# Queries and values of an edge-attention layer made by one 256-column product in three rotating PSUM banks

## What is computed

```python
Xq = (H @ W_lin.T).reshape(bt, n, h, dh)
Xv = (H @ W_val.T).reshape(bt, n, h, dh)
e = jnp.einsum('behd,hd->beh', jax.nn.leaky_relu(Xq[:, src] + Xq[:, dst], 0.2), a)
e = e + jnp.log(A0[src, dst] + EPS)[None, :, None]
# softmax of e over the edges of each source node gives attn
Vt = Xv[:, dst].transpose(1, 0, 2, 3)
Y = jax.ops.segment_sum(attn[..., None] * Vt, src, num_segments=n)
return Y.transpose(1, 0, 2, 3).reshape(bt, n, d) @ W_out.T
```

## Time and profile before

| | us |
|---|---|
| median of 3 runs | 1201.16 |
| lowest to highest | 1200.19 to 1201.65 |
| the profiled execution | 1202.18 |
| its span, first to last instruction | 1200.4 |
| TensorE busy in the span | 1161.4 |
| VectorE busy | 991.0 |
| ScalarE busy | 817.9 |
| mean granted TensorE clock | 0.994 |

### The profile page before, as it was taken

One profiled execution on the slowest core, in us unless ns is written; L12 is line 12 of the kernel. 1 busy time (PEld: TensorE's weight loads), 2 busy tenths in 40 slices (PEclk: granted clock), 3 DMA queues, 4 the chain that ended last, 5 costly groups with the idle time before them and its releaser, 6 DMA issues. The chain is left out here.

```text
span 1200.4 us, 23784 instructions
## 1 busy us (share of the span) xinstructions
PE 1161.4 (97%) x7820; PEld 1021.9 (85%) x7820; DVE 991.0 (83%) x2791; ACT 817.9 (68%) x1826; POOL 387.9 (32%) x717
## 2 busy tenths in 40 slices
PE   5999999999999999999998999989999999999998
PEld 4798898998988989889897898877777798889997
DVE  5888988888889888898886899988877689976665
ACT  4685886868868768588685777757777777753332
POOL 4211100100001001010011677756666487742332
PEclk9999999999999999999998999999999999999999
DMA  9400000000000000000000000000000000002222
GB/s 261 121 1 1 1 2 0 0 0 0 0 0 0 0 0 0 0 0 0 1 1 1 2 2 2 2 1 1 2 1 1 1 2 1 2 3 69 71 69 73
DMA packets 26306, 20.85 MB, mean 17 GB/s; under 512 B 1776, under 2 KB 22256, under 8 KB 26224
## 3 DMA queue, kind: packets, MB, share of 16 engines
q1 hardware_dynamic: 25648, 19.68, 5.8%
q10 hardware_dynamic: 576, 0.13, 0.1%
HBM read 11.42 MB, written 8.39 MB: 17 GB/s over the span
## 5 line engine op out<-in xcount | busy, mean ns | idle before, releaser
L554 ACT ACTIVATE gate<-ps,b_lstm 128x256 f32<-128x256 f32 (+2 forms) x624 | 309.5, 564 | 94.4 <-PE ps L581 92.9
L579 PE MATMUL ps<-H_hi,w_hi 128*128 128x256 f32 (+2 forms) x624 | 210.3, 338 | 1.9 <-DVE H_lo L470 1.2
L580 PE MATMUL ps<-H_hi,w_lo 128*128 128x256 f32 (+2 forms) x624 | 205.1, 330 | 0.0
L581 PE MATMUL ps<-H_lo,w_hi 128*128 128x256 f32 (+2 forms) x624 | 193.2, 330 | 0.0
L131 POOL TENSOR_SCALAR rstd<-mv 128x8 f32<-128x8 f32 x16 | 5.0, 311 | 500.3 <-DVE mv L111 500.1
L579 PEld LDWEIGHTS ps<-H_hi,w_hi 128*128 128x128 f32 x624 | 117.7, 189 | 15.8 <-DVE H_lo L470 3.2
L580 PEld LDWEIGHTS ps<-H_hi,w_lo 128*128 128x128 f32 x624 | 117.9, 189 | 8.1
L581 PEld LDWEIGHTS ps<-H_lo,w_hi 128*128 128x128 f32 x624 | 115.4, 189 | 10.1 <-DVE H_lo L508 1.5
L579 PE MATMUL ps<-hid_hi,w_hi 128*128 128x256 f32 (+2 forms) x384 | 120.5, 320 | 0.3
L580 PE MATMUL ps<-hid_hi,w_lo 128*128 128x256 f32 (+2 forms) x384 | 116.8, 311 | 0.0
L561 ACT ACTIVATE tanh_c<-cell 128x512 f32<-128x512 f32 (+2 forms) x176 | 90.9, 516 | 24.5 <-DVE cell L498 17.4
(11 more groups left out here) (205 smaller groups left out, 3095.6 us busy)
## 6 DMA issues: line engine op xcount, KB each, us to landing
out<-x SPq DMA_DIRECT2D x32, 256.0 KB, 2.3
x<-in_WihT SPq DMA_DIRECT2D x1, 768.0 KB, 11.3
x<-in_WhhT SPq DMA_DIRECT2D x1, 768.0 KB, 6.0
x<-in_x_in SPq DMA_DIRECT2D x2, 256.0 KB, 3.6
x<-in_x_in SPq DMA_DIRECT2D x1, 512.0 KB, 7.9
x<-in_WihT SPq DMA_DIRECT2D x1, 256.0 KB, 8.2
tanh_c<-in_WqkvT SPq DMA_DIRECT2D x1, 192.0 KB, 5.0
w_sb<-in_W SPq DMA_DIRECT2D x1, 192.0 KB, 4.2
```

The source lines that it names most:

```text
L554: nc.scalar.activation(gate[:, g, z, 0:w * GB], gate_bank(g, k, m)[:, 0:w * GB], ACT.Tanh if z == G else ACT.Sigmoid, bias=b_lstm[:, 4 * ( ...
L579: nc.tensor.matmul(dst, w_hi[:, src, p - 1, z], v_hi, start=start, stop=False)
L580: return nc.tensor.matmul(dst, w_lo[:, src, p - 1, z], v_hi, start=False, stop=False)
L581: return nc.tensor.matmul(dst, w_hi[:, src, p - 1, z], v_lo, start=False, stop=stop)
```

## The change

For each batch one product with the whole w_lv (256 columns: queries, then values) takes the place of two with 128. A bank holds two batches; a group takes two banks of the three banks 1 to 3, in turn. Gather moves to banks 4 and 5, logits to 6, values to 0 and 2, y to 1, the output to 4. One semaphore `d_xp` stands for `d_xqp` and `d_xvp`. The query copy waits for it; the value copy comes behind `relu_hT(n + 1)` and waits for `d_xql`, VectorE's subtraction. Where a group's two banks do not lie side by side (n % 3 = 1) each of the three readers works in two instructions. The first product of a group waits for the value copy of group n - 2, the third for that of n - 1.

```diff
-        logit_rows = ps[:, 5, 0:E]
-        def query_bank(n):
-            return ps[:, (1, 6)[n % 2]]
+        logit_rows = ps[:, 6, 0:E]
+        def bank_of(n, b):
+            return 1 + (2 * n + b // 2) % 3
+        def pieces(n):
+            if n % 3 == 1:
+                return [(slice(b, b + 2), ps[:, bank_of(n, b)].rearrange("p (b c) -> p b c", b=2)) for b in (0, 2)]
+            return [(slice(0, QB), ps[:, bank_of(n, 0):bank_of(n, 0) + 2].rearrange("p k (b c) -> p (k b) c", b=2))]
+        VALUE_BANK, Y_BANK, OUT_BANK = (0, 2), 1, 4
...
                     dve.wait_ge(S["d_xqh"], n + 1)
-                    nc.vector.tensor_tensor(xq_lo[:, n % 2], by4(query_bank(n)), xq_hi[:, n % 2].bitcast(F32),
-                                            ALU.subtract).then_inc(S["d_xql"], 1)
+                    for of, two in pieces(n):
+                        ins = nc.vector.tensor_tensor(xq_lo[:, n % 2, of], two[:, :, 0:C],
+                                                      xq_hi[:, n % 2, of].bitcast(F32), ALU.subtract)
+                    ins.then_inc(S["d_xql"], 1)
...
-                    act.wait_ge(S["d_xqp"], n + 1)
+                    act.wait_ge(S["d_xp"], n + 1)
                     if n > 1:
                         act.wait_ge(S["d_zp"], (n - 1) * 2)
-                    nc.scalar.activation(xq_hi[:, n % 2], by4(query_bank(n)), ACT.Copy).then_inc(S["d_xqh"], 1)
-                    act.wait_ge(S["d_xvp"], n + 1)
-                    nc.scalar.activation(xv[:, n * QB:n * QB + QB], by4(ps[:, 2]), ACT.Copy).then_inc(S["d_xv"], 1)
+                    for of, two in pieces(n):
+                        ins = nc.scalar.activation(xq_hi[:, n % 2, of], two[:, :, 0:C], ACT.Copy)
+                    ins.then_inc(S["d_xqh"], 1)
                     if n + 1 < NG:
                         relu_hT(n + 1)
+                    act.wait_ge(S["d_xql"], n + 1)
+                    for of, two in pieces(n):
+                        ins = nc.scalar.activation(xv[:, n * QB + of.start:n * QB + of.stop], two[:, :, C:2 * C], ACT.Copy)
+                    ins.then_inc(S["d_xv"], 1)
...
                     pe.wait_ge(S["d_hT"], n + 1)
-                    if n > 1:
-                        pe.wait_ge(S["d_xql"], n - 1)
                     for b in range(QB):
-                        ins = nc.tensor.matmul(query_bank(n)[:, b * C:(b + 1) * C], hT3[:, b], w_lv[:, 0:C],
+                        if b == 0 and n > 1:
+                            pe.wait_ge(S["d_xv"], n - 1)
+                        if b == 2 and n > 0:
+                            pe.wait_ge(S["d_xv"], n)
+                        ins = nc.tensor.matmul(ps[:, bank_of(n, b), b % 2 * 2 * C:(b % 2 + 1) * 2 * C], hT3[:, b], w_lv[:],
                                                start=True, stop=True)
-                    ins.then_inc(S["d_xqp"], 1)
-                    if n > 0:
-                        pe.wait_ge(S["d_xv"], n)
-                    for b in range(QB):
-                        ins = nc.tensor.matmul(ps[:, 2, b * C:(b + 1) * C], hT3[:, b], w_lv[:, C:2 * C],
-                                               start=True, stop=True)
-                    ins.then_inc(S["d_xvp"], 1)
+                    ins.then_inc(S["d_xp"], 1)
```

More of the change, by code:

```diff
@@ L1076, in four_layers @@
         near = tmp("near", [P, EC])
-        S = sync_names(nc, ctx, "d_stats d_aggr d_var d_rstd d_nmean d_shift d_hn d_hTp d_hT d_xqp d_xvp d_xqh d_xql "
+        S = sync_names(nc, ctx, "d_stats d_aggr d_var d_rstd d_nmean d_shift d_hn d_hTp d_hT d_xp d_xqh d_xql "
                                 "d_xv d_zp d_rl d_lr d_lgp d_near d_loga d_logp "
@@ L1196, in leaky @@
                         nc.vector.scalar_tensor_tensor(
-                            lr[:, n % LRS, 2 * k:2 * k + 2].rearrange("p b e -> p (b e)"), ps[:, 3 + k], SLOPE, rl[:, k],
+                            lr[:, n % LRS, 2 * k:2 * k + 2].rearrange("p b e -> p (b e)"), ps[:, 4 + k], SLOPE, rl[:, k],
                             ALU.mult, ALU.add).then_inc(S["d_lr"], 1)
@@ L1240, in weigh @@
                                 va[:, c, k * HB:(k + 1) * HB].rearrange("p b (h d) -> p (b h) d", h=HEADS),
-                                ps[:, c, k * HB * C:(k + 1) * HB * C].rearrange("p (n d) -> p n d", d=DH),
+                                ps[:, VALUE_BANK[c], k * HB * C:(k + 1) * HB * C].rearrange("p (n d) -> p n d", d=DH),
                                 att[:, c, cols:cols + HB * HEADS].unsqueeze(2).to_broadcast([P, HB * HEADS, DH]),
@@ L1247, in finish @@
                     dve.wait_ge(S["e_op"], n + 1)
-                    nc.vector.tensor_tensor(xs, xs, by4(ps[:, 3]), ALU.add).then_inc(S["e_o"], 1)
+                    nc.vector.tensor_tensor(xs, xs, by4(ps[:, OUT_BANK]), ALU.add).then_inc(S["e_o"], 1)
                 weigh(0)
@@ L1262, in relu_hT @@
                     if n > 0:
-                        act.wait_ge(S["d_xvp"], n)
+                        act.wait_ge(S["d_xp"], n)
                     nc.scalar.activation(hT3[:], by4(ps[:, 0]), ACT.Relu).then_inc(S["d_hT"], 1)
@@ L1286, in relu_part @@
                             act.wait_ge(S["d_lr"], n * 2 - 1 + k)
-                        nc.scalar.activation(rl[:, k], ps[:, 3 + k], ACT.Relu, scale=1.0 - SLOPE).then_inc(
+                        nc.scalar.activation(rl[:, k], ps[:, 4 + k], ACT.Relu, scale=1.0 - SLOPE).then_inc(
                             S["d_rl"], 1)
@@ L1314, in copy_y @@
                         act.wait_ge(S["e_op"], n)
-                    nc.scalar.activation(y3, by4(ps[:, 2]), ACT.Copy).then_inc(S["e_y"], 1)
+                    nc.scalar.activation(y3, by4(ps[:, Y_BANK]), ACT.Copy).then_inc(S["e_y"], 1)
                 high_values(1)
@@ L1375, in gather @@
                         for b in range(2):
-                            dst = ps[:, 3 + k, b * E:(b + 1) * E]
+                            dst = ps[:, 4 + k, b * E:(b + 1) * E]
                             nc.tensor.matmul(dst, xq_hi[:, n % 2, 2 * k + b], hot_sd[:], start=True, stop=False)
@@ L1418, in values @@
                     pe.wait_ge(S["e_xvl"], n + 1)
+                    if n == 0:
+                        pe.wait_ge(S["d_xv"], NG - 1)
                     if n > 0:
@@ L1421, in values @@
                     for c in range(EC):
-                        nc.tensor.matmul(ps[:, c], hot_d[:, c * P:(c + 1) * P], xv_hi[:], start=True, stop=False)
-                        nc.tensor.matmul(ps[:, c], hot_d[:, c * P:(c + 1) * P], xv_lo[:], start=False,
+                        nc.tensor.matmul(ps[:, VALUE_BANK[c]], hot_d[:, c * P:(c + 1) * P], xv_hi[:], start=True,
+                                         stop=False)
+                        nc.tensor.matmul(ps[:, VALUE_BANK[c]], hot_d[:, c * P:(c + 1) * P], xv_lo[:], start=False,
                                          stop=True).then_inc(S["e_vp"], 1)
                 def aggregate(n):
-                    if n > 0:
+                    if n == 0:
+                        pe.wait_ge(S["d_xv"], NG)
+                    else:
                         pe.wait_ge(S["e_y"], n)
@@ L1432, in aggregate @@
                         for c in range(EC):
-                            ins = nc.tensor.matmul(ps[:, 2, b * T:(b + 1) * T], va[:, c, b], hot_sT[:, c],
+                            ins = nc.tensor.matmul(ps[:, Y_BANK, b * T:(b + 1) * T], va[:, c, b], hot_sT[:, c],
                                                    start=(c == 0), stop=(c == EC - 1))
@@ L1440, in project @@
                     for b in range(QB):
-                        ins = nc.tensor.matmul(ps[:, 3, b * C:(b + 1) * C], y3[:, b], w_out[:], start=True, stop=True)
+                        ins = nc.tensor.matmul(ps[:, OUT_BANK, b * C:(b + 1) * C], y3[:, b], w_out[:], start=True, stop=True)
                     ins.then_inc(S["e_op"], 1)
```

## The result

| | before | after |
|---|---|---|
| median, us | 1201.41 (4 runs) | 1210.80 (4 runs) |
| lowest to highest | 1200.19 to 1202.30 | 1209.21 to 1212.36 |
| the profiled execution | 1202.18 | 1212.36 |
| its span | 1200.4 | 1210.5 |

The changed kernel is slower: ratio 1.0076, 95% interval 1.0064 to 1.0088, that is 9.4 us with an interval of 7.7 to 10.6. The page, part 1, of the changed kernel, to be set beside the earlier trace rows: TensorE's busy time grew by 2.4 us in a span 10.1 us longer, VectorE's and ScalarE's by 0.2 and 0.3. So no engine got noticeably more work; they wait more.

A forecast was written before the change was run, and what follows sets the result against it. TensorE and VectorE, nearly full and waiting for each other in the edge-logits stage, bound the kernel; 5.55 us between bursts, 1.8 ahead of the first and 1.35 at the end made 8.7, so 1210.0 us by the median (1203.5 to 1214.5).

The forecast's parts named there:

- Bound and chain: Edge-logits stage: TensorE and VectorE nearly full and waiting for each other through gather, ScalarE's relu, VectorE's leaky, next gather.
- Record of the wide product: TensorE's 256-column product records: 0.217 us apart, a group 0.05 us less, 1.6 us over 32 groups.
- Rival (b): Wide record costs TensorE much less than two narrow ones: faster, 1194.9 us by the gather's pace; chance 0.05.
- Query copy late by 0.8 us: ScalarE's query copy starts 1.93 us after the products start instead of 1.14, and VectorE's subtraction slips with it.
- Value copy ahead of the relu: On ScalarE's queue the value copy waits for the subtraction and stands ahead of the next relu, which also waits.
- Table loads: Ln's and first Exp's 1.28 us loads queue behind the value copy, holding the relu by 1.5 and 1.2 us.
- End: Last gather of the stage: its relu comes behind the last value copy, 1.35 us later.
- Bank turn: A group's third product waits for the previous group's value copy: 3.92 against 4.05 us, free by 0.1 us.
- rival (c): Late value copies hold the third product: 0.65 us per split group, 7 us more, 1216.9 us; chance 0.08.
- Split copies: Query copy, subtraction and value copy in halves in 11 of 32 groups: 0.1 us charged for each split instruction.
- Signs: Profile marks expected in the stage, such as longer waits for query copy and gather, and marks of being wrong.
- Rival (a): VectorE's slack behind each burst takes up the 0.8 us: not slower, 1199.6 us; chance 0.11.

The follow-up runs named there:

- e1: Kernel before with only the query copy late, waiting for all eight products, and the value copy behind the hT copy without a new wait; 1208.14 us.
- e7: Changed kernel with the query copy of every group in two halves by bank, the first after two of four products; 1207.29 us.
- e8: Changed kernel with each 256-column product made as two of 128 columns, its banks, waits and splits kept; 1212.69 us.
- c1_changed_again: The changed kernel as it is, run and profiled once more; 1210.46 us, ratio 1.0072 to the kernel before.
- e2: Kernel before with only the value copy moved behind the hT copy and waiting for VectorE's subtraction, query copy as early as before; 1203.57 us.
- e6: Changed kernel with the Ln and the Exps put ahead of the value copy's wait; 1207.99 us.
- e9: Changed kernel with query copy in halves by bank, Ln and Exps ahead of the value copy's wait, relu_part(30) ahead of the last value copy; 1205.19 us.
- e5: Changed kernel with the value copy one place further on, behind relu_part of the next iteration; 1221.52 us.
- e4: Kernel before with only the copies and subtraction split into halves of 256 columns for n % 3 = 1; 1202.08 us.
- e3: Kernel before with late query copy and value copy waiting for the subtraction, still 128-column products, old banks, no splits; 1209.58 us.

## Why the prediction was right

It said 1210.0 us in a range of 1203.5 to 1214.5, slower with 0.82; measured 1210.8.

- **Bound and chain.** Two engines nearly full, tied by gather, relu, leaky. Shown: delays of VectorE or ScalarE by a few tenths of a us came out in the sections (e1, e7), in e1 with no engine's work changed.
- **Record of the wide product.** It was taken at 0.217 us, measured 0.216 (1.73 us for eight). The saving was put at 1.6 us; e8 shows 1.1. The likely reason, not tested by itself, is that where VectorE is late the shorter product ends in a wait. The prediction also weighed the rule of the page "TensorE: Matmul & The Clock Gate" of the Trainium skill, section "Back-to-back issue gap", that the weight load sets the spacing of small products as well. This case doesn't bear it out: with half the weight loads a record of 256 columns takes 0.216 us where two of 128 take 0.224, so 0.008 and not the 0.025 by which the prediction's estimate of 6.4 us went. Rival (b) fell.
- **Query copy late by 0.8 us.** Shown by e1, and by dose in e7. The growth of the six sections, all causes together, was put at 0.8, 0.8, 1.3, 0.95, 0.9, 0.8 (5.55); c1_changed_again less the kernel before gives 0.76, 0.74, 1.21, 0.86, 0.71, 0.70 (4.98).
- **Value copy ahead of the relu.** Right in its places. Alone it costs 1.7 us (e2); on top of the late query copy 135.9 - 133.9 = 2.0.
- **Table loads.** The Exp's was put at 0.4 and gives 0.37 back in e6. The part ahead of the first burst was put at 1.8 and is 2.0 in c1_changed_again, of which e6 gives 1.1 back.
- **End.** Put at 1.35, measured 1.27; e9 takes it away.
- **Bank turn and rival (c).** Free "by 0.1 us" was nearly right. One sign of being wrong that the prediction names, TensorE waiting inside the products for `xv`, did come, in three groups: the weight load of the third product waits 0.26 us there, the records start 0.13 us late, 0.4 us in the whole stage. (The prediction's 3.2 + 0.87 is 4.07, not 4.05.) e5 shows what lay behind that margin: with the value copy one place later the stage loses more than the 7 us that rival (c) had been given. **Split copies**: charged 0.1 us for each of three instructions in 11 groups, though some of it falls beside other work; e4 shows 0.4 us in all, and the changed kernel's ScalarE timeline has 0.66 us for two halves and 0.60 for one.
- **Signs.** VectorE's wait for the query copy was put at about 20 us and is 16.3; TensorE's wait at the gather was to grow by 9 us in most iterations and grew by 7.9, in 12 of 32 gathers, so not in most; the wait of 2 us ahead of the last gather came as put (2.04).
- **Sum.** It was 8.7 us; the stage grew by 135.7 - 127.4 = 8.3 without the half-clock stretch. The prediction's median should read 1209.9 (1201.16 + 8.7) where it says 1210.0, which changes nothing. Rival (a), that VectorE's slack takes up the delay, is out: its slack lies ahead of leaky, and the subtraction behind it.

From the parts, e3 with e4 added and e8 taken off leaves 8.5 + 0.4 - 1.1 = 7.8 against 8.3. The bank turn can be at most 0.4 of these 0.5 us, by the record starts above; no run separates it. The mechanism was right and the sizes nearly so. That the total came so close is helped by errors of both signs: the sections were put 0.6 us too high, the part ahead of the first burst 0.2 too low.

Why can the query copy not start earlier in this layout? With queries and values in one bank, ScalarE would read while TensorE writes the same bank. The page "PSUM — Partial Sum Buffer" of the Trainium skill, section "PSUM bank collisions raise a hardware error", says that two engines on one bank and quadrant (32 partitions) collide and that the chip doesn't make them wait. The kernel's semaphores keep to that, and no run here tried it. e7 goes as far as that rule allows, by whole banks.

## What to carry to other kernels

In this kernel joining two products saved TensorE at most what the distance between its records says (0.06 us a group), but it moves the first result to the end of the joined product; if a reader of the first half heads a chain that two engines wait for, that delay is paid once for every time the chain starts anew (here once a section, behind each burst). Price a merged product by who reads its first half and when, and by what the shared bank makes take turns. When a copy is moved back in an in-order queue, list everything that gets behind it, table loads first.

## What was not expected

A wait between two products of one group is hardly absorbed, though TensorE waits elsewhere in the section anyway: in e5 it came to 0.6 us a group, 2.4 us a section, and the sections grew by 1.2 to 1.9 us, since product, copy and subtraction all sit behind it. And executions of one kernel differ in where TensorE runs at half clock: the first profile of the changed kernel had a stretch of it (0.53 of full clock from 948 to 950 us) behind idle times of 1.12 and 0.69 us, while c1_changed_again had the same idle times and full clock. That moved the stage by 1.6 us, a sixth of what the profiles of before and after differ by.
